# Masked graph products: two units at a time instead of four, one row step everywhere, a short second pass, end rows shared anew

## The reference

```python
rel_ids = jnp.arange(1, weight.shape[0] + 1, dtype=relation.dtype)        # 1, 2, 3, 4
masks = (relation[None] == rel_ids[:, None, None, None]).astype(x.dtype)
h = jnp.einsum('rbnm,bmd->rbnd', masks, x)
y = jnp.einsum('rbnd,rdo->bno', h, weight) + bias
x = _layernorm(x + y, axis=-1)
```

## Time and profile before

| what | value |
|---|---|
| median of 3 runs | 120.71 us |
| profiled execution | 120.54 us |
| its span | 118.8 us |
| PE busy (matmuls) | 106.6 us, 90% |
| ACT busy | 88.1 us, 74% |
| DVE busy | 84.8 us, 71% |
| POOL busy | 70.3 us, 59% |
| load and store queue (q1) | 41.49 MB, 88.6% of 16 engines |
| chain that ended last | PE 58%, DMA 29%, SP's queue 5%, DVE 2% |

### The profile page before, as it was taken

The page is one execution under the profiler, slowest core; times in us unless marked ns, Lnnn a source line. Parts: engine busy times, 40 slices in busy tenths (PEclk is TensorE's granted clock), DMA queues, the critical chain, the costliest instruction groups (busy, mean ns, idle before and its releaser), DMA issues.

```text
span 118.8 us, 2879 instructions
## 1 busy us (share of the span) xinstructions
PE 106.6 (90%) x1012; PEld 80.4 (68%) x1023; DVE 84.8 (71%) x252; ACT 88.1 (74%) x114; POOL 70.3 (59%) x132
## 2 busy tenths in 40 slices
PE   6788999899999979999999999999999999999400
PEld 2168898799997646767676767676868676679300
DVE  1055678397877848696959887787779777998840
ACT  4088277947797999799999499968987698925530
POOL 2007001940047998399569955995689577977740
PEclk9999999999999999999999999999999999999985
DMA  3999999999999999999999999999999999450271
GB/s 73 389 408 411 414 407 422 414 391 412 425 414 384 419 403 436 380 414 414 419 391 404 422 406 394 420 406 423 377 433 411 415 399 383 141 177 0 85 248 35
DMA packets 12419, 42.22 MB, mean 355 GB/s; under 512 B 882, under 2 KB 7155, under 8 KB 8947
## 3 DMA queue, kind: packets, MB, share of 16 engines
q1 hardware_dynamic: 12256, 41.49, 88.6%
q10 hardware_dynamic: 146, 0.52, 1.3%
HBM read 37.81 MB, written 4.19 MB: 354 GB/s over the span
## 4 chain that ended last, share of the span: by engine, by line
PE 58%; DMA 29%; SPq 5%; DVE 2%; issue 1%; ACT 0%; DVEq 0%
PE h_ps L619 32%; DMA adj_sb<-adj 29%; PE ids_t L601 16%; PE y_ps L633 9%; SPq L396 4%; PE ids_t L633 1%; DVE x_sb L758 0%; SPq L393 0%; SPq L412 0%; ACT std L539 0%; DVE stats L711 0%; DVE x_sb L705 0%; DVE moments L717 0%; DVEq L255 0%; DVE shift L751 0%
## 5 line engine op out<-in xcount | busy, mean ns | idle before, releaser
L522 ACT ACTIVATE junk<-adj_sb,minus 128x2048 bf16<-128x2048 int32 x32 | 63.8, 1994 | 0.4 <-DMA adj_sb<-adj 0.4
L699 DVE TENSOR_SCALAR mask_t<-ids_t 128x1024 bf16<-128x1024 uint16 x64 | 43.6, 687 | 25.2 <-PE ids_t L601 24.1
L601 PEld LDWEIGHTS ids_t<-ident,adj_sb 128*128 128x128 bf16 x512 | 36.5, 123 | 13.8 <-DMA adj_sb<-adj 2.7
L601 PE MATMUL ids_t<-ident,adj_sb 128*128 128x128 bf16 x512 | 40.0, 221 | 2.3 <-DMA adj_sb<-adj 2.2
L619 PE MATMUL h_ps<-mask_t,x_lo 128*128 128x512 bf16 (+2 forms) x184 | 33.5, 314 | 0.0
L619 PE MATMUL h_ps<-mask_t,x_hi 128*128 128x512 bf16 (+2 forms) x173 | 31.1, 310 | 1.2 <-DVE mask_t L699 0.6
L448 POOL TENSOR_TENSOR x_lo<-x_sb,x_hi 128x1024 f16<-128x1024 f32 x7 | 15.0, 2144 | 24.2 <-ACT x_hi L531 24.2
L488 POOL TENSOR_SCALAR x_sb<-x_sb,rstd,shift 128x128 f32<-128x128 f32 x55 | 24.0, 457 | 1.0
L535 ACT ACTIVATE h_all<-h_ps 128x512 f32<-128x512 f32 (+2 forms) x23 | 10.6, 463 | 18.1 <-PE h_ps L619 18.1
L454 POOL TENSOR_TENSOR x_sb<-x_sb,bias_sb 128x1024 f32<-128x1024 f32 x8 | 19.0, 2377 | 7.8 <-DVE x_lo L764 7.7
L619 PEld LDWEIGHTS h_ps<-mask_t,x_hi 128*128 128x128 f16 x184 | 15.6, 98 | 7.2 <-DVE mask_t L699 1.2
(11 more groups left out here) (44 smaller groups left out, 30.8 us busy)
## 6 DMA issues: line engine op xcount, KB each, us to landing
adj_sb<-adj SPq DMA_DIRECT2D x27, 1024.0 KB, 19.5
adj_sb<-adj SPq DMA_DIRECT2D x10, 512.0 KB, 8.4
x_sb<-x SPq DMA_DIRECT2D x7, 512.0 KB, 18.9
out<-x_sb SPq DMA_DIRECT2D x7, 512.0 KB, 16.7
x_sb<-x ACTq DMA_DIRECT2D x1, 512.0 KB, 5.4
out<-x_sb SPq DMA_DIRECT2D x2, 256.0 KB, 3.3
w_sb<-weight SPq DMA_DIRECT2D x1, 64.0 KB, 6.1
bias_row<-bias ACTq DMA_DIRECT2D x1, 0.5 KB
```

What stands on the lines that cost most here:

```text
L522: nc.scalar.activation(junk[:, at % 2], adj_sb[:, slot, 2 * k:2 * k + 2, :], ACT.Square, scale=2.0, bias=minus[:, 0:1], accum_out=squares[ ...
L601: last = nc.tensor.transpose(bank[:, j, :], words[:, j // step(b), j % step(b), 0, :], ident[:, :])
L699: nc.vector.tensor_scalar(mask_t[:, b % 2, :, u * P:(u + 1) * P], ids_t[u % T_BANKS][:, :, :].bitcast(UINT16), 1.0, None, ALU.mult).then_i ...
```

## The change

Step by step:

- **Groups.** Batches 0 and 1 are cut into two groups of 4 units like the others. Group 0's products are made one unit at a time; those of the other groups two units at a time, so 8 matmuls of 256 columns for `x_hi` and 8 for `x_lo` per two units.
- **Order on PE.** The units that are transposed between the products of a group are its own last two and then the next group's first two.
- **Loads.** One row step of 2 in all batches. Batch 1 is loaded in single units. x of batch 0 comes in two halves on SP's queue behind unit (0,0), where ACT's queue issued it before; x of the following batch is issued ahead of the last pair of a batch, not behind it.
- **ACT.** Checks are dealt out two a group, three in groups 6 and 7.
- **End.** d's x is added by PE (`add_x`, a matmul with an fp32 identity), so DVE takes d's statistics from PSUM and `sum_rows` of d goes. The instruction for `shift` of the last set goes. POOL normalises 2 of its units, ACT none, DVE 2. Of batch 6's rows POOL has 3 and ACT 5 (4 and 4 before). `find_far` and `find` stand behind the last mask, as before.
- **POOL.** `normalise` subtracts the mean and multiplies, so `minus_mean` and `shift` are made for two sets only.
- **Second pass.** Rewritten as a loop over single units with fp32 matmuls: 44 matmuls in PE's loop body where there were 288.

```diff
     def split(b):
-        if b == 0:
-            return [(0, 1), (1, 1), (2, 2), (4, 2), (6, 2)]
-        if b == 1:
-            return [(0, 2), (2, 2), (4, 2), (6, 2)]
         return [(0, 4), (4, 2), (6, 1), (7, 1)] if b == B - 1 else [(0, 4), (4, 4)]
...
-        first = [1, 2, 2, 3, 4, 5, 6, 7, 8, 11, 13]
+        first = [2, 4, 6, 8, 10, 12, 15]
         if g.index < len(first):
             return first[g.index]
-        return min(PAIRS * (g.b + 1) + (2 if ends_batch(g) else 0), PAIRS * B)
+        return min(2 * g.index + 4, PAIRS * B)
...
             load_unit(0, 0)
+            for n in range(2):
+                sp.dma_start(units_of(x_sb[:, 0], n * HALF, HALF), rows_of(x, 0, n * HALF, HALF)).then_inc(s_x0[n], 16)
             load_unit(0, 1)
...
-            load_unit(1, 0)
             load_x(1)
-            load_unit(1, 1)
-            for k in range(1, PAIRS):
-                load_adj(1, k)
-            load_x(2)
+            for u in range(J):
+                if u == 6:
+                    load_x(2)
+                load_unit(1, u)
             for b in range(EARLY, B):
                 for k in range(PAIRS):
+                    if k == PAIRS - 1 and b + 1 < B:
+                        load_x(b + 1)
                     load_adj(b, k)
-                if b + 1 < B:
-                    load_x(b + 1)
...
-            for g in groups[2:LAST + 1]:
-                coming = coming_after(g)
-                for n, u in enumerate(coming):
-                    transpose_unit(groups[g.index + 1].b, u)
-
-                    if n == (len(coming) - 1 if g.index < LAST else 1):
+            for g in groups[1:LAST + 1]:
+                n = groups[g.index + 1]
+                for units, coming in ((g.units[:2], [(g.b, u) for u in g.units[2:]]),
+                                      (g.units[2:], [(n.b, u) for u in n.units[:2]])):
+                    transpose_unit(*coming[0])
+                    products(g, units, x_hi)
+                    transpose_unit(*coming[1])
+                    products(g, units, x_lo)
+                    if units[0] == g.first:
                         project(groups[g.index - 1])
-                    products(g, n, len(coming))
...
+            products(d, d.units, x_hi)
+            products(d, d.units, x_lo)
             project(e)
+            add_x(d)
             project(d)
```

More of the change, by code:

```diff
@@ L230, in adj_resnorm_kernel @@
         g_root = [sem(f"g_root{n}") for n in range(4)]
[L232 to L242, removed]
+        ids = adj_sb[:, 1, 0, 0:N // 2].bitcast(BF16).rearrange("p (j q) -> p j q", q=P)
+        masks = mask_t[:, 0].bitcast(FP32).rearrange("p j q -> p (j q)").rearrange("p (r j q) -> p r j q", r=R, q=P)
+        row_of_x, xb, result = (x_sb[:, n, 0, :] for n in (1, 2, 3))
+        x_v, adj_v, out_v = (t.rearrange("b (k p) d -> b p k d", p=P) for t in (x, adj, out))
         def wait_for_stores(engine):
@@ L305, in second_pe @@
             with pe.Fori(0, B) as b:
[L306 to L312, removed]
+                with pe.Fori(0, J) as u:
+                    pe.wait_ge(g_cast, J * b + u + 1)
+                    for j in range(J):
+                        last = nc.tensor.transpose(ids_t[0][:, j, :], ids[:, j, :], ident[:, :])
+                    last.then_inc(g_tr, 1)
+                    pe.wait_ge(g_x, 16 * (b + 1))
+                    pe.wait_ge(g_mask, J * b + u + 1)
+                    for r in range(R):
@@ L318, in second_pe @@
+                    last.then_inc(g_prod, 1)
+                    pe.wait_ge(g_h, J * b + u + 1)
                     for r in range(R):
[L319 to L326, removed]
-                                    h_ps[r % 2][:, :], part[:, j, :], halves(masks[:, j, :], r % 2),
-                                    start=(j == 0 and n == 0), stop=(j == J - 1 and n == len(parts) - 1))
@@ L618, in products @@
+                cols = slice(units[0] * P, (units[-1] + 1) * P)
+                for j in range(J):
+                    if g.index == 0 and units[0] == 0 and j % HALF == 0:
                         pe.wait_ge(((s_hi0, s_hi) if part is x_hi else (s_lo0, s_lo))[j // HALF], 1)
-                    last = nc.tensor.matmul(h_ps[g.bank][:, 0:g.count * P], part[:, g.b % 2, j, :],
-                                            mask_t[:, g.b % 2, j, g.cols], start=(j == 0 and part is x_hi),
-                                            stop=(j == J - 1 and part is x_lo))
@@ L622, in products @@
-                if hi == len(todo):
+                    last = nc.tensor.matmul(h_ps[g.bank][:, to], part[:, g.b % 2, j, :], mask_t[:, g.b % 2, j, cols],
+                                            start=(j == 0 and part is x_hi), stop=(j == J - 1 and part is x_lo))
+                if part is x_lo and units[-1] == g.units[-1]:
                     last.then_inc(s_prod, 1)
@@ L687, in _ @@
             s_worst = sem("worst_ready")
[L688 removed]
+            s_n = [sem(f"root{n}") for n in range(3)]
             def row_maxima(b):
```

384 lines of the change are left out of this document (175 added, 209 removed).

## The result

| kernel | median | span of the profiled execution |
|---|---|---|
| before | 120.61 us (120.49 to 120.75, 4 runs) | 118.8 us |
| changed | 122.81 us (122.46 to 122.95, 4 runs) | 121.0 us |

The ratio is 1.0177, with a 95% interval of 1.0152 to 1.0203. The change makes the kernel 1.8% slower, where 1.6% faster was forecast. The changed kernel's profiled execution took 122.95 us.

The account below looks back on a forecast made before the run. Loads bound the early part, then PE without gaps, then the end's branch and store. Gains of 0.7 us (PE's and DVE's order) and 1.2 (branch and store) took 120.5 to 118.6, plus 0.17: 118.7 us, range 118.0 to 119.9.

Parts of the forecast that it names:

- POOL's two units take some 0.5 each: Last set of rows: POOL's two normalise units at some 0.5 us each, against DVE's two at 0.66; 0.3 us lost.
- Slower: Rival, 9%: DVE's masks over 0.45 us late in every group, so PE waits in each; 122.0 us at 0.3 a group.
- The front: Early loads: two x loads in 1 KB pieces cost 0.2 us each, so (2,0) lands at 32.2 instead of 31.8.
- PE's arrival: Start of batch 2: PE is just ready for unit (2,0) when its load lands, both at 32.2 us.
- PE from there: Groups after (2,0) lands: 6.23 us each without load waits, so group a's products end at 103.6, 1.8 us sooner.
- just hidden: ACT's copy of group 7's result: done at 62.5 us, PE wants it at 62.7; charged 0.
- The end: After a's products: last mask starts unchanged at 105.4, later steps save 0.84 us, POOL loses 0.3; last store issued 0.7 sooner.
- The branch and the store: Kernel's finish: PE's second-pass branch under 0.1 us instead of 4.31, store 2.6, then 0.7 to the span's end at 116.9.
- The branch still fetches: Rival, 17%: PE's branch over the second pass still waits for instructions or its transfer delays the store; 119.3 or 120.0 us.
- the 1.2 us: Share of the 1.9 us forecast gain assigned to the branch over the second pass and the last store.

Follow-up runs that it names:

- b_step2: The kernel before with row step 2 in batches 0 and 1 too, so their x is read in 1 KB pieces instead of 4 KB; 122.34 us, 1.0111 of before.
- a_pool_old_x0_act: The changed kernel with POOL's old multiply-and-add form except in the last set, and x of batch 0 issued whole by ScalarE's queue; 119.92 us, 0.9916 of before.
- a_step8: The changed kernel with POOL's old form, last set adding minus the mean, x of batch 0 on ScalarE's queue, row step 8 in batches 0 and 1; 118.12 us, 0.9798.
- a_long_second: The changed kernel with POOL's old form, last set adding minus the mean, and the old second pass of 288 matmuls; 120.55 us, 1.0006 of before.
- b_pool_forms: The kernel before with a different form of POOL's normalise in each of six batches; 122.4 us, one run.
- b_short_second: The kernel before with the changed kernel's short second pass alone; 120.85 us, 0.9996 of before.
- b_pool_new: The kernel before with POOL's new normalise alone (subtract the mean, multiply by rstd); 126.55 us, 1.0472 of before.
- a_pool_old: The changed kernel with POOL's old multiply-and-add normalise for all sets but the last; 119.91 us, 0.9936 of before.

## Why the prediction was wrong, step by step

**The step that failed** is in the part on the end: "POOL's two units take some 0.5 each", and with it what the prediction left out. The change section lists that `normalise` subtracts the mean and multiplies, and the prediction charges nothing for it. It took the new form's time to be the old form's. With a subtraction a unit takes 0.80 us where it took 0.45, 2.8 us more a batch. POOL had that much free on average, at 59% busy, but it left nothing over in the string of one batch: split, roots, eight units, `add_bias`. The full 12.3 us equal PE's period, and with POOL full what made it late stayed: `add_bias` of the last batch ended at 108.93, 2.0 us behind the time at which group a's sum was forecast, and POOL's string at the end came 2.7 us behind VectorE. With the old form for all sets but the last 2.9 us of span come back, and 0.6 more in the last set. No rival named POOL. "Slower" stood at 9% and for another reason, the masks. In the changed kernel PE's matmuls in the groups never waited for a mask; one weight load did, for 0.8 us.

**The front** was mis-sized. The term of 0.2 us for each x load in 1 KB pieces came from loads in the steady part. The row step costs 1.7 us until (2,0) (`b_step2`), not 0.4. PE's arrival was right: with the step undone PE begins (2,0) at 32.25 us against 32.2 forecast. That the load landed at 32.2 there too is luck in part, for by my terms it was due at 31.8 without the 0.4. Whether the place of x of batch 0 adds a little to it, `a_pool_old_x0_act` could not tell apart from nothing.

**PE from there** was right: 6.18 us a group against 6.23. 256-column products cost what was worked out. ACT's copy of group 7, "just hidden", did not hold PE.

**The end** was right in its parts where POOL is not in it. In `a_step8` the sum of group a starts at 106.47, where 106.9 was forecast.

**The branch and the store.** The branch was right in kind: 0.24 us, where under 0.1 was said and 4.3 had stood. "The branch still fetches" is refuted. The store was taken as 2.6 us, from other stores than the last, and took 2.1, and from its landing to the end of the span 0.5 us passed where 0.7 was taken; before's last store, at 3.9 us, is not among the prediction's rows. So the 1.2 us are not the branch's gain alone. The kernel before with the short second pass gains nothing (0.9996), the changed kernel without it loses 1.4%. What decides as well, as far as the traces tell, is whether a transfer of instructions falls into the last store: the last store took 3.4 to 3.9 us where one of 16 KB did, 2.1 to 2.3 where none did.

**The sum.** In the spans of profiled executions: 121.0 for the changed kernel; 118.1 with POOL's old form; 117.5 with the last set's too; 117.2 with x of batch 0 on ScalarE's queue; 115.9 with the row step. The forecast was 116.9, with 0.4 for the row step in it. The last is from the fastest of six executions; their median span is 116.3. So the change without its two costly side edits, the form on POOL and the row step, is worth about what was forecast. The order on PE, two units at a time, was not run by itself: `a_long_second`, which has it with the long second pass and the row step, is as fast as before (1.0006).

## What to carry to other kernels

An edit that reads as algebra, (x - mean) * rstd for x * rstd + shift, is a new instruction on its engine. If the trace has no row of it, its price is not known, and what it may cost more is to be multiplied by the count of a whole period before it is called hidden: here 0.35 us times 8 filled an engine whose average was 59%. Where two things end together, look for what the second one waits for before the first is priced: a branch that is gone gave nothing in one kernel and 1.4% in another.

## What the runs showed of the hardware

- **POOL's subtraction.** POOL's TENSOR_SCALAR on 128x128 fp32, with two operands that hold one value for each partition, takes 796 to 798 ns with a subtraction in it and 448 to 455 with multiply and add alone (`b_pool_forms`).
- **Transfers of instructions on the DMA engines.** In the changed kernel 10 of 16 are 16 KB, and such a one takes about 1 us (0.96 in `b_short_second`); the others are 8 KB. Where one of 16 KB fell into the last store of 256 KB, one to three of the store's 16 parts were late, and it took 3.4 to 3.9 us to landing (`a_long_second`, before) in place of 2.1 to 2.3 (changed kernel, `b_pool_new`). That the two shared a DMA engine is inferred. The Trainium skill (Runtime: NRT & Kernel Launch, "Instruction fetch mechanics") says that an engine's instructions come in blocks of 16 KiB through a DMA queue of the sequencer's own, and that the cost of crossing from one block to the next is mostly hidden. The trace agrees with the size for those 10; in the last store it was, by this reading, not hidden.
- **A VectorE operation that ended with POOL's.** In the changed kernel one small operation took 0.88 us:

```profile
108.07 0.88 DVE L734 SCALAR_TENSOR_TENSOR worst<-odd,high 128x1 f32<-128x1 f32 x1
```

It ended at 108.95, and POOL's `add_bias` at 108.93. In `a_pool_old`, where POOL's `add_bias` was over by then, it took 0.20. The Trainium skill (SBUF — State Buffer, "Who interferes with whom") says that a VectorE instruction with two inputs in SBUF contends with a GpSimd instruction that reads SBUF, and that the port pair the two share is an exclusive lock. This one has two such inputs, so the trace agrees, in the one instance that I looked at. It cost 0.2 us at most, as group a's sum had to wait for the same `add_bias` and started 0.23 us behind its end.
